# Two halves of an attention weight in one 32-bit word, masked in place after the subtraction

## The reference

```python
def _agnn(x, a, beta):
    x_norm = x / jnp.clip(jnp.linalg.norm(x, axis=-1, keepdims=True), EPS, None)
    scores = beta[0] * (x_norm @ x_norm.T)
    scores = jnp.where(a > 0, scores, NEG_INF)
    attn = jax.nn.softmax(scores, axis=-1)
    return attn @ x
h = jnp.maximum(_layernorm(x, axis=-1), 0.0)
x = x + _L0_gnn_ref(h, adj, ...)          # hyperbolic graph layer
h = jnp.maximum(_layernorm(x, axis=-1), 0.0)
h = _leaky(_agnn(h, adj, beta1))          # attention layer 0
h = _leaky(_agnn(h, adj, beta2))          # attention layer 1
x = x + h
```

## Time and profile before

| | us |
|---|---|
| median of 3 runs | 1070.74 (1069.54 to 1072.2) |
| profiled execution | 1071.25 |
| its span | 1069.7 |
| TensorE matmul busy | 990.1 (93%) |
| VectorE busy | 929.9 (87%) |
| ScalarE busy | 679.1 (63%) |
| GpSimd busy | 34.0 (3%) |

### The profile page before, as it was taken

How to read it: one execution, slowest core, us unless ns; L and a number is a source line. 1 busy time by engine, 2 the same in 40 slices (tenths; PEclk the granted TensorE clock), 3 DMA queues, 4 the chain that set the end, 5 groups by cost and what they waited for, 6 DMA issues and landing times.

```text
span 1069.7 us, 24266 instructions
## 1 busy us (share of the span) xinstructions
PE 990.1 (93%) x8672; PEld 665.3 (62%) x8672; DVE 929.9 (87%) x2276; ACT 679.1 (63%) x894; POOL 34.0 (3%) x31
## 2 busy tenths in 40 slices
PE   2889999999977699999999999969999999999995
PEld 2754444444445377777777777737777777777774
DVE  7692888888899979999999999958899899998996
ACT  2721112111234478889889898858888888888784
POOL 0000000000013500000000000000000000000000
PEclk9889999999998899999999999989999999999998
DMA  9228998888852346556555666616566665666600
GB/s 306 100 84 286 299 287 281 281 283 279 279 170 102 119 159 194 191 175 195 195 193 193 196 196 196 190 49 201 193 207 197 204 205 187 211 198 194 208 23 13
DMA packets 107231, 206.44 MB, mean 193 GB/s; under 512 B 3632, under 2 KB 8368, under 8 KB 107184
## 3 DMA queue, kind: packets, MB, share of 16 engines
q1 hardware_dynamic: 105536, 203.44, 59.2%
q0 software_dynamic: 640, 2.10, 0.6%
q10 hardware_dynamic: 1008, 0.33, 0.1%
HBM read 203.75 MB, written 2.10 MB: 192 GB/s over the span
## 4 chain that ended last, share of the span: by engine, by line
PE 54%; DVE 6%; issue 3%; ACT 1%; DVEq 0%; POOL 0%; ACTq 0%; POOLq 0%
PE s_ps L410 25%; PE acc_ps L426 10%; PE acc_ps L430 10%; PE acc_ps L428 9%; DVE h_all L1037 3%; DVE work L1030 1%; DVE t L1054 1%; DVE t L1062 1%; PE s_ps L351 0%; ACT work L638 0%; ACT t L677 0%; ACT t L660 0%; ACT h_all L645 0%; DVE set L906 0%; ACT t L666 0%
## 5 line engine op out<-in xcount | busy, mean ns | idle before, releaser
L638 ACT ACTIVATE work<-s_ps,beta_bias,beta_scale 128x1024 f32<-128x1024 f32 x256 | 307.1, 1200 | 91.3 <-PE s_ps L410 91.3
L1030 DVE SCALAR_TENSOR_TENSOR work<-ring,work 128x1024 f32<-128x1024 f32 x256 | 319.9, 1250 | 44.2 <-ACT work L638 41.7
L1037 DVE TENSOR_TENSOR h_all<-work,h_all 128x1024 f16<-128x1024 f32 x244 | 297.5, 1219 | 3.1 <-ACT h_all L645 2.8
L645 ACT ACTIVATE h_all<-work 128x1024 f16<-128x1024 f32 x256 | 268.3, 1048 | 33.6 <-DVE work L1030 33.2
L364 PE MATMUL acc_ps<-ring,set 128*128 128x512 f32 x512 | 225.6, 600 | 3.1 <-DVE set L888 3.1
L426 PE MATMUL acc_ps<-src,h_all 128*128 128x129 f16 x1024 | 186.2, 222 | 18.0 <-POOL h_all L276 9.9
L410 PE MATMUL s_ps<-set 128*128 (+1 forms) x768 | 187.5, 381 | 4.1 <-issue 3.1
L410 PE MATMUL s_ps<-xt 128*128 (+1 forms) x768 | 189.0, 384 | 0.8 <-DVE xt L906 0.4
L430 PE MATMUL acc_ps<-src,h_all 128*128 128x129 f16 x1024 | 186.3, 224 | 0.0
L428 PE MATMUL acc_ps<-src,h_all 128*128 128x128 f16 x1024 | 185.9, 222 | 0.0
L426 PE MATMUL acc_ps<-set,h_all 128*128 128x129 f16 x1024 | 182.4, 219 | 3.3 <-DVE h_all L1037 3.3
(11 more groups left out here) (186 smaller groups left out, 710.2 us busy)
## 6 DMA issues: line engine op xcount, KB each, us to landing
ring<-in_adj_t SPq DMA_DIRECT2D x192, 1024.0 KB, 5.3
x_sb<-in_x SPq DMA_DIRECT2D x4, 512.0 KB, 8.2
out<-x_sb POOLq DMA_DIRECT2D x8, 256.0 KB, 2.9
w<-in_layer ACTq DMA_DIRECT2D x2, 64.0 KB, 6.2
w<-in_embed ACTq DMA_DIRECT2D x1, 64.0 KB, 2.6
eb<-in_embed_bias ACTq DMA_DIRECT2D x1, 64.0 KB, 5.2
lb<-in_layer_bias ACTq DMA_DIRECT2D x1, 64.0 KB, 7.0
beta<-in_beta ACTq DMA_DIRECT2D x2, 0.5 KB, 6.4
```

Of the source, the lines that this page charges most:

```text
L638: nc.scalar.activation(e_ring[:, t % ER, :], s_ps[:, t % 2, :], ACT.Exp, bias=beta_bias[:, la:la + 1], scale=beta_scale[:, la:la + 1])\
L645: nc.scalar.activation(ph_ring[:, t % LAG, :], m_ring[:, t % LAG, :], ACT.Copy)\
L1030: V.scalar_tensor_tensor(m_ring[:, t % LAG, :], ring[:, k, half_tile:half_tile + SB, :] .rearrange("p b i -> p (b i)"), 0.0, e_ring[:, t % ...
L1037: V.tensor_tensor(pl_ring[:, t % LAG, :], m_ring[:, t % LAG, :], ph_ring[:, t % LAG, :], ALU.subtract).then_inc(pl_done[la], n)
```

## The change

The f32 ring of masked weights, `m_ring`, goes. A tile of weights is now 1024 words of 32 bits per partition; seen as f16 pairs, element 0 of each word is the low half, element 1 the high half. There are WR = 8 such tiles, four in the memory of the old f16 rings (`h_all`) and four in that of the old `m_ring`. ScalarE copies the unmasked e into the high halves; VectorE (GpSimd in the first 12 steps) subtracts and writes the low halves; then VectorE masks the whole word, taken as f32, in place: a word times 1.0 keeps its bits, times 0.0 becomes zero in both halves. The weighted sum reads each half as stationary operand with a step of two elements, and waits for the mask. exp(t) now waits for p_lo(t-2) in place of mask(t-2), since p_lo is the last reader of `e_ring`. LAG stays at four.

```diff
+    WR = 8
-        p_rings = h_all[:, 0:LAG * SB * CH].bitcast(f16).rearrange("p (s r n) -> p s r n", s=2, r=LAG)
-        ph_ring, pl_ring = p_rings[:, 0], p_rings[:, 1]
-        work = sb("work", [P, (ER + LAG) * SB * CH])
+        work = sb("work", [P, (ER + WR // 2) * SB * CH])
-        m_ring = work[:, ER * SB * CH:(ER + LAG) * SB * CH].rearrange("p (r n) -> p r n", r=LAG)
+        w_low = h_all[:, :].rearrange("p (r n) -> p r n", r=WR // 2)
+        w_high = work[:, ER * SB * CH:(ER + WR // 2) * SB * CH].rearrange("p (r n) -> p r n", r=WR // 2)
+        words = [(w_low, w_high)[i * 2 // WR][:, i % (WR // 2), :] for i in range(WR)]
+        halves = [w.bitcast(f16).rearrange("p (n s) -> p s n", s=2) for w in words]
+        WORD_LO, WORD_HI = 0, 1
...
                 for t in range(PAUSES):
                     pool.wait_ge(ph_done[0], t + 1)
-                    wait(pool, pv_done[0], t + 1 - LAG)
-                    pool.tensor_tensor(pl_ring[:, t % LAG, :], m_ring[:, t % LAG, :], ph_ring[:, t % LAG, :],
-                                       ALU.subtract).then_inc(pl_early, 1)
+                    pool.tensor_tensor(halves[t % WR][:, WORD_LO, :], e_ring[:, t % ER, :],
+                                       halves[t % WR][:, WORD_HI, :], ALU.subtract).then_inc(pl_early, 1)
...
-                wait_p_lo(pe, la, c * NS + (t + 1), joined)
+                pe.wait_ge(mask_done[la], c * NS + (t + 1))
+                w_hi, w_lo = halves[t % WR][:, WORD_HI, :], halves[t % WR][:, WORD_LO, :]
...
             def exps(la, c, t, shifted, joined=False):
                 act.wait_ge(s_done[la], c * NS + (t + 1))
-                wait(act, mask_done[la], c * NS + (t + 1 - ER))
+                wait_p_lo(act, la, c * NS + (t + 1 - ER), joined)
...
+            def p_hi(la, c, t, shifted):
+                act.wait_ge(e_masked[la] if shifted else exp_done[la], c * NS + (t + 1))
+                wait(act, pv_done[la], c * NS + (t + 1 - WR))
+                nc.scalar.activation(halves[t % WR][:, WORD_HI, :], e_ring[:, t % ER, :], ACT.Copy)\
                     .then_inc(ph_done[la], 1)
...
+            def mask(la, c, t, joined=False):
+
+                wait_p_lo(dve, la, c * NS + (t + 1), joined)
+                w = words[t % WR]
+                V.scalar_tensor_tensor(w, mask_in(la, c, t), 0.0, w, ALU.is_gt, ALU.mult).then_inc(mask_done[la], 1)
+
+            def p_lo(la, c, t, shifted, n=1):
+
                 dve.wait_ge(ph_done[la], c * NS + (t + 1))
-                wait(dve, pv_done[la], c * NS + (t + 1 - LAG))
-                V.tensor_tensor(pl_ring[:, t % LAG, :], m_ring[:, t % LAG, :], ph_ring[:, t % LAG, :],
-                                ALU.subtract).then_inc(pl_done[la], n)
+                V.tensor_tensor(halves[t % WR][:, WORD_LO, :], e_ring[:, t % ER, :], halves[t % WR][:, WORD_HI, :],
+                                ALU.subtract).then_inc(mask_done[la] if shifted else pl_done[la], n)
...
-                    mask(la, c, t, t0 > 0)
...
                     if t > t0:
-                        p_lo(la, c, t - 1, 1 + t0 if t == t0 + 1 else 1)
+                        p_lo(la, c, t - 1, shifted, 1 + t0 if t == t0 + 1 else 1)
                     elif not first:
-                        p_lo(la, c - 1, NS - 1)
+                        p_lo(la, c - 1, NS - 1, shifted)
+                    if not shifted:
+                        if t:
+                            mask(la, c, t - 1, t0 > 0)
+                        elif not first:
+                            mask(la, c - 1, NS - 1)
```

More of the change, by code:

```diff
@@ L174, in build @@
         mask_done = [sem(f"mask_done{i}") for i in range(2)]
+        e_masked = [sem(f"e_masked{i}") for i in range(2)]
         ph_done = [sem(f"ph_done{i}") for i in range(2)]
@@ L212, in __call__, with wait_p_lo @@
                 self.eng.wait_ge(self.s, self.base + self.n)
-        def wait_p_lo(eng, la, n, joined):
+        def wait_p_lo(eng, la, n, joined=False):
             if joined and n <= PAUSES:
@@ L415, in scores, with weighted_sum @@
                 last.then_inc(s_done[la], 1)
[L417 to L419 removed]
+            def weighted_sum(la, c, t):
+                pe.wait_ge(mask_done[la], c * NS + (t + 1))
+                w_hi, w_lo = halves[t % WR][:, WORD_HI, :], halves[t % WR][:, WORD_LO, :]
                 if t == 0:
@@ L425, in weighted_sum @@
                         col = ts(u * CB + b, P)
-                        nc.tensor.matmul(acc_ps[:, b, 0:PW], ph_ring[:, t % LAG, col], src[la][:, jb, F:AW],
+                        nc.tensor.matmul(acc_ps[:, b, 0:PW], w_hi[:, col], src[la][:, jb, F:AW],
                                          start=jb == 0, stop=False)
-                        nc.tensor.matmul(acc_ps[:, b, 0:F], ph_ring[:, t % LAG, col], src[la][:, jb, 0:F],
+                        nc.tensor.matmul(acc_ps[:, b, 0:F], w_hi[:, col], src[la][:, jb, 0:F],
                                          start=False, stop=False)
-                        last = nc.tensor.matmul(acc_ps[:, b, 0:PW], pl_ring[:, t % LAG, col],
+                        last = nc.tensor.matmul(acc_ps[:, b, 0:PW], w_lo[:, col],
                                                 src[la][:, jb, F:AW], start=False, stop=jb == NB - 1)
@@ L466, in chunk @@
                     if t >= LAG:
-                        weighted_sum(la, c, t - LAG, joined)
+                        weighted_sum(la, c, t - LAG)
                     elif t >= TAIL[la] and not first:
@@ L481, in chunk @@
                 for t in range(TAIL[la]):
-                    weighted_sum(la, c, NS - LAG + t, joined)
+                    weighted_sum(la, c, NS - LAG + t)
                 if first:
@@ L628, in _, with exps @@
             asks_gnn = start + NC * ASKS_CHUNK
-            def exps(la, c, t, shifted):
+            def exps(la, c, t, shifted, joined=False):
                 if shifted:
@@ L640, in exps @@
                     .then_inc(exp_done[la], 1)
-            def p_hi(la, c, t):
-                act.wait_ge(mask_done[la], c * NS + (t + 1))
-                wait(act, pv_done[la], c * NS + (t + 1 - LAG))
-                nc.scalar.activation(ph_ring[:, t % LAG, :], m_ring[:, t % LAG, :], ACT.Copy)\
+            def p_hi(la, c, t, shifted):
+                act.wait_ge(e_masked[la] if shifted else exp_done[la], c * NS + (t + 1))
+                wait(act, pv_done[la], c * NS + (t + 1 - WR))
+                nc.scalar.activation(halves[t % WR][:, WORD_HI, :], e_ring[:, t % ER, :], ACT.Copy)\
                     .then_inc(ph_done[la], 1)
@@ L689, in chunk @@
                         split_columns(1, c - 1, slot_ps)
-                    exps(la, c, t, shifted)
+                    exps(la, c, t, shifted, t0 > 0)
                     if la == 0 and not first and t == NS - 3:
@@ L695, in chunk @@
                     if t:
-                        p_hi(la, c, t - 1)
+                        p_hi(la, c, t - 1, shifted)
                     elif not first:
-                        p_hi(la, c - 1, NS - 1)
+                        p_hi(la, c - 1, NS - 1, shifted)
                     if not first and t == LAG:
@@ L708, in between @@
             def between(i):
-                exps(0, 0, i + 1, False)
+                exps(0, 0, i + 1, False, True)
                 if i >= 0:
-                    p_hi(0, 0, i)
+                    p_hi(0, 0, i, False)
                 if i == 1:
@@ L727, in attention @@
                     chunk(la, c, False, shifted)
-                p_hi(la, NC - 1, NS - 1)
+                p_hi(la, NC - 1, NS - 1, shifted)
                 sums_leave(la, NC - 1)
@@ L1187, in between @@
             def between(i):
-                mask(0, 0, i, True)
+                if i > 0:
+                    mask(0, 0, i - 1, True)
             def attention(la, shifted):
@@ L1204, in attention @@
                     chunk(la, c, False, shifted)
-                p_lo(la, NC - 1, NS - 1)
+                p_lo(la, NC - 1, NS - 1, shifted)
+                if not shifted:
+                    mask(la, NC - 1, NS - 1)
                 averages(la, NC - 1)
```

20 lines of the change are left out of this document (9 added, 11 removed).

## The result

| | before | after |
|---|---|---|
| median, us | 1071.1 (1069.54 to 1072.2, 4 runs) | 1390.33 (1387.05 to 1392.87, 4 runs) |
| span of the profiled execution, us | 1069.7 | 1385.5 |
| granted clock, mean | 0.972 | 0.968 |

The ratio of the times is 1.298, with a 95% interval of 1.2948 to 1.3012. The forecast was 1277 us, in a range up to 1318. The direction was right, the size was not: 113 us more were lost than forecast.

The account below looks back on a forecast made before the run. TensorE set the pace before, at 2.67 us a step; the change would make a 3.44 us loop through ScalarE and VectorE. 187.6 + 11.7 + 4.2 + 2 = 205.5 us on 1071.25 gave 1277 us, range 1257 to 1318.

Parts of the forecast that it names:

- The loop: Each step: exp(t), p_hi(t-1), p_lo(t-1), exp(t+1) run without overlap through ScalarE and VectorE, 3.44 us against TensorE's 2.67; chance 0.83.
- Costs that no row of before shows: Strided halves and in-place mask: p_lo kept at 1.22 us, p_hi at 1.05 (bound 1.20), weight loads unchanged.
- The hand-over back: From VectorE's subtraction to ScalarE's next exp, in every step: 0.04 us.
- Other work in the loop: Per-chunk work beside the steps: 0.50, 1.18 and 0.83 us in layer 0, 0.50 and 0.55 in layer 1.
- The sums' leaving: The sums leave PSUM between exp(2) and p_hi(1) on ScalarE: 0.50 us on the loop per chunk.
- the normalised rows: Layer 0's rows stand between exp(13) and p_hi(12) on ScalarE: 1.18 us on the loop per chunk.
- layer 0's chunk end: Transposes, two weighted sums, then scores delay exp(0) to 4.27 us after exp(15) instead of 3.44: 0.83 us.
- Layer 1's whole-row operations on VectorE: Two per chunk hold VectorE 1.45 us, 0.55 beyond its spare 0.9.
- Strided loads: Rival: interleaved weight loads bound TensorE, step 3.99 us, 1406 us in all; chance 0.04.
- Slower writers: Rival: strided halves slow p_hi and p_lo, 25.6 us per 0.1 us, 1315 up to about 1510 us; chance 0.07.
- The clock: Rival: TensorE's clock falls in the new 0.77 us gaps, 1740 us if at the lower level throughout; chance 0.01.
- mask(t-4) is long done: In each step, the weighted sum four steps behind finds its mask finished, so TensorE is no part of the loop.

Follow-up runs that it names:

- e3: The changed kernel with ScalarE's copy of tile t issued directly behind exp(t), ring of two exponential tiles kept: 1106.65 us, ratio 1.0358.
- e1: The changed kernel with each tile's two halves side by side instead of interleaved, so both are written without a stride; output differs: 1288.71 us, ratio 1.2057.
- e8: The changed kernel with high halves contiguous in their own unmasked tiles, only low halves interleaved, four tiles of each; output differs: 1307.84 us, ratio 1.2225.
- e9: The changed kernel with single copies, subtractions and hand-overs measured behind its end, no other engine at work: 1506.52 us for the whole, one run.
- e10: The changed kernel with turns of exp, copy, subtraction behind its end: alone, with a mask, with a second wait on the exp: 1449.02 us, one run.
- e4: The kernel before with only its high and low halves interleaved as f16 pairs; order, waits and mask as before: 1089.22 us, ratio 1.0177.
- e5: The changed kernel with four exponential tiles instead of two, four word tiles instead of eight, and the copy directly behind its exp: 1095.40 us, ratio 1.0234.

## Why the forecast was right in kind and wrong in size

- **The loop: right.** Exp, copy, subtraction, exp is what the timelines show, 226 of the 256 exps are released by the subtraction (1.46 to 1.50 us of idle in the turn above, 1.2 forecast), and undoing one link (e3) returns 283.7 us.
- **Costs that no row of before shows: this step failed.** It took p_hi at 1.05 us and p_lo at 1.22 as if a strided half were written like a contiguous one. They measured 1.35 and 1.30 to 1.35. The upper bound for the copy was read from the exp, 1.20, a different operation with a contiguous output; it was no bound for this. With e1 and e8: some 77 us for the copy and 25 for the subtraction, 101.6 together.
- **The hand-over back: 0.04 taken, 0.09 measured** in the loop, about 12 us. The 0.04 came from a mask that released a copy; e9 and e10 found 0.03 to 0.04 for the loop's own pair as well when nothing else ran.
- **Other work in the loop: nearly right.** The sums' leaving gave steps of 4.39 us (0.49 more; 0.50 forecast), as 526.61 to 531.00 shows below; the normalised rows gave seven steps of 5.03 (1.13 more; 1.18 forecast). At layer 0's chunk end exp(0) starts 4.19 us after exp(15) (450.16 to 454.35), forecast 4.27; above the slower loop's 3.90 that is only 0.29 more instead of 0.83. Layer 1's whole-row operations on VectorE, priced at 0.55 a chunk, cost at most 0.1: apart from the sums' step none of its later chunks has a step above 4.01 us.

```profile
526.61 1.21 ACT L641 ACTIVATE work<-s_ps,beta_bias,beta_scale 128x1024 f32<-128x1024 f32 x1 [1.43 <-DVE h_all L1048]
...
531.00 1.20 ACT L641 ACTIVATE work<-s_ps,beta_bias,beta_scale 128x1024 f32<-128x1024 f32 x1 [1.43 <-DVE h_all L1048]
```

- **The account,** by the start of the copy that moves a chunk's sums out (L653, before L650), in the two profiled executions. Up to layer 0's first: 398.84 against 391.70, 7.1 us more where 2 were forecast, so 5.1 above forecast. From there to layer 0's last, 848.40 against 695.70: 145.6 more, forecast 96.6 + 2.1, so 46.9. From there to layer 1's first, 936.94 against 760.64: 23.6 more, forecast 11.7, so 11.9. From there to layer 1's last, 1375.52 against 1059.76: 139.5 more, forecast 91.0 + 2.1, so 46.4. Together 110.3 us, all by which the profiled execution of 1387.05 us exceeds the forecast's 1276.75; the median lies 3 us higher. The two large terms are each 112 steps x 0.46 = 51.5 us, less what the forecast had too much at the chunk ends.
- **Strided loads: rightly low.** Loads 99 to 101 ns, weighted matmuls 58 ns apart, in the changed kernel and in e4. The rule of the Trainium skill ("TensorE: Matmul & The Clock Gate", weight-path perf modes) that fast weight load reads two 16-bit weights at a time did not turn into a doubled load here.
- **The rule on 16-byte lines** ("SBUF — State Buffer" of the Trainium skill, section on the DMA port swizzle) says that up to eight bf16 may be strided free. The trace disagrees for writes (ScalarE's copy, e9): 1.34 us at a stride of two, 2.47 at four, 4.73 at eight against 1.06. It agrees for the subtraction's read at two. The measurement decides. I had let this rule confirm the 1.05 and 1.22.
- **Slower writers, at 0.07, was the true rival.** Its price per 0.1 us (25.6 us) was right: (0.30 + 0.08 to 0.13) x 256 = 97 to 110, measured 101.6. "Nothing in the rows speaks for it" was true, and no ground for 0.07: the rows said nothing at all about strided writes.
- **The clock: a trace of it,** and not where the short gaps are. At each of layer 0's seven chunk ends TensorE stands idle for 2.2 us before the transposes (L353). Behind three of these idles the granted clock fell from 2.4 GHz: to a mean of 0.66 in 640 to 645 and in 705 to 710 us, where no exp came late, and to 0.55 and 0.77 in the two halves of 770 to 780 us, where the weighted matmuls went from 58 to 107 ns apart, the scores came late, and a step that takes 4.19 us at the other chunk ends took 5.93. It fell once more behind an idle of 3.72 us in layer 1's first chunk (0.50, the lower level, 1.2 GHz, in 925 to 930 us), and a step took 5.88 us. The two steps cost about 4 us. The forecast had given the clock 0.01, for gaps of 0.77 us and throughout; the loop's own gaps of 1.1 us a step left it at 1.00, and the longer idles at the chunk ends and in the first chunk had no place in it.

```profile
772.40 1.20 ACT L641 ACTIVATE work<-s_ps,beta_bias,beta_scale 128x1024 f32<-128x1024 f32 x1 [1.05 <-DVE work L1048]
...
778.33 1.20 ACT L641 ACTIVATE work<-s_ps,beta_bias,beta_scale 128x1024 f32<-128x1024 f32 x1 [3.48 <-PE s_ps L412]
```

TensorE before each of the two late steps, and the window around the first:

```profile
769.72 0.66 PE L353 MATMUL s_ps<-ident,t 128*128 128x128 f32 x4 [2.22 <-ACT work L641]
...
924.88 2.74 PE L412 MATMUL s_ps<-set 128*128 x6 [3.72 <-ACT col_sums L685]
```

```profile
770.00:780.00 10.00, 9.12 (x76) 7.01 (x75) 6.38 (x6) 5.47 (x6) 0.00 (x0) 0.66 0.33 105
```

- **"mask(t-4) is long done" was wrong,** without a price: the mask ends at 611.10 + 1.23 = 612.33 and the weighted sum behind it starts at 612.39. The scores behind that still landed at 613.78 + 1.46 = 615.24, well ahead of the exp that reads them, at 619.01. Nor does the mask start 0.16 us after its own subtraction, as was taken: it starts 0.03 us after (614.98 to 615.01). That had no price either, since the mask is outside the loop.
- **No version of the word form beat the kernel before.** The best of those that leave nothing out is e5, 1095.4 us. Before, TensorE is full, and the change takes nothing off it.

## What to carry to other kernels

Write the dependences of a buffer ring as a cycle with program order in it: a ring of two whose last reader moves one engine further back can join two engines into one chain, and swapping two neighbours in one engine's program may cut it, for 284 us here. Where no row shows an operation's access pattern, price it from a measurement of that pattern; the price of a neighbour with another pattern is no upper bound. In a closed chain each such error counts in full at every turn: the same slower writers cost 101.6 us inside it and 18.8 outside.
